# Layer 0's expert network in 240 pieces between the attention's steps, in a two-layer transformer kernel

## The chip, the cores and the metric

The kernel runs on one core of one Trainium2 chip. The metric is the device time of one execution in microseconds (us). TensorE (PE) multiplies, its weight loads (PEld) overlap its products; VectorE (DVE), ScalarE (ACT) and GpSimd (POOL) work on what it leaves; SP issues most DMAs. A line number L1673 is a line of the kernel before; L1673 is the helper in which nearly every product is issued, so TensorE's rows are told apart by their tiles.

## The reference, cut to what matters

Two layers act on x of 2 x 1024 tokens of 128 values. Each normalises x, computes an attention s and an expert network g from the same normalised xn, and adds s * silu(g). Layer 0, cut:

```python
xn = _layernorm(x, axis=-1)
s = _L0_attn_ref(xn, ...)     # 16 heads of 8, 1024 x 1024 scores, relative bias, softmax, projection
g = _silu(_L0_ffn_ref(xn, ...))
x = x + s * g
# the expert network: 2 shared experts and 8 routed ones, all computed for all tokens,
# 128 -> 256 -> 128, the routed ones weighted with the top-2 gate
def _ffn(x, w1, w2, w3):
    return jax.nn.silu(x @ w1.T) * (x @ w3.T) @ w2.T
```

Layer 1 has another attention and a larger expert network, which the change doesn't touch but for the numbers of banks, written as a table by layer.

## The kernel before

**Layout.** Features lie on the 128 partitions, tokens along the free axis; `xnT` holds xn so, in four chunks of 512 tokens. PSUM has 8 banks of 512 float32 per partition.

**Start (L1964 to L1972).** Transposes, the projections to q, k and v, and the router. q and k are split into three bf16 parts each and stored to DRAM by SP (`store_qk`, L563), from where stacks of 48 rows (six part-by-part products of 8) are loaded per group of four heads (`load_stacks`, `load_group`). Meanwhile VectorE makes the bias rows (L1520 to L1527, stored at L657) and the gate (L1530 to L1533).

**The expert stage (L2013 on TensorE).** Ten experts in order, each over the four chunks, with two halves of 128 hidden values: 8 units per expert, 80 in all. A unit is `up` (L1975): for w1 and for w3 three float32r products (high by high, high by low, low by high) of 512 columns in two banks, of four in use; ScalarE's Silu of the first (L1002); VectorE's product with the second (L1548); for routed experts GpSimd's product with the gate row (L867); and `down` (L1984), a float32 product added in one of banks 4 to 7, one per chunk. At unit 4 of each expert ScalarE and VectorE split the next expert's weights (L1006, L1515). The loops are `ffn_experts` (L497) on all engines. At the end ScalarE takes Silu of the four banks into `n1T` (L1014).

**The attention (`attention(0)` on each engine).** Two batches with four groups of four heads are eight groups; each is done in two halves H of 512 queries, 16 halves in all. It needs two passes. The *score units* (S) compute 128 queries by 512 keys and VectorE takes their maximum (L1442); 32 of them per half. They go through a ring of banks 0 to 3 (`RING`, `ring_unit` at L1767). When a half's maxima are complete (mark K, L1434), GpSimd splits them in parts (L810 to L813), TensorE transposes them (unit M), VectorE copies them (L1447) and SP writes them as three more rows of the q stack (`max_rows`, L597). The *transposed pass* of a half has 8 steps of 128 keys: per step four products T (128 keys by 512 queries, one per head, `st_step`) with 51 rows, in banks 4 to 6 in turn, whose exponential ScalarE takes (L943), and the value product of the step before (`av_step`, eight float32 passes into four column groups of bank 7). Heads alternate between array rows 0 to 63 and 64 to 127. For some query tiles the bias is added by small bf16 products (`s_adds`, `st_adds`, with `flip`).

The order is written out by a planner (`s_stream`, `s_plan`, L117 to L169): 52 score units and a K and an M come before the first step (`first_units`), and the others are dealt over the steps, those of later halves into the steps of earlier ones. Within a step TensorE issues T and a share of the units for each of the four heads, and the value product behind the third T. All engines run the same lists in order; waits are on counters (`ring_full`, `ring_free`, `st_ps`, `e_done`, `av_done`).

After each half the sums go out and back through DRAM (`sums_out`, `sums_back`, SP) and GpSimd multiplies (`normalise`, L819). SP's order of this is `attention_feed` (L623). In the last half, without score units, TensorE begins the output projection (`first_projection`, L1906); VectorE's `projected` (L1556) multiplies it by `n1T` and adds it to xT.

Of the kernel before, what the change touches and what calls it, by code (L numbers as in the profile page):

```python
# [51 lines left out]
RING = 4  # L52
EXP = 8
FFN_SEQ = EXP + 2
REL = 249
# [32 lines left out]
def s_units(layer, H):  # L88
# [10 lines left out]
    return out  # L99

# [119 lines left out]
def block_net(nc, a, out):  # L220
    ctx = ExitStack()
    with ctx:
# [13 lines left out]
        drev_dram = dram("drev_dram", (GROUPS, HG, 2, PARTS, DREV), BF16)  # L236
# [44 lines left out]
        with ExitStack() as over:  # L281
# [3 lines left out]
            part("below_x_hi", 8, F32)  # L285
            x_hi = part("x_hi", 8)
            part("below_x_lo", 8, F32)
            x_lo = part("x_lo", 8)
            part("below_xe", 32, F32)
# [5 lines left out]
            part("below_g", 4, F32)  # L295
            g_hi_lo = part("g_hi_lo", 16)
# [11 lines left out]
        q_at = [4 * G for G in range(GROUPS)]  # L308
        k_at = [48, 52, 56, 60, 32, 36, 40, 44]
        Qs = [bf(k, 4).rearrange("p (r t) -> p r t", r=PAIRS) for k in q_at]  # L310
        Ks = [bf(k, 4).rearrange("p (r t) -> p r t", r=PAIRS) for k in k_at]
# [12 lines left out]
        lrow = at(140, 2)  # L324
# [14 lines left out]
        def gate_bufs(n):  # L339
# [14 lines left out]
        cwb = at(100, 16).rearrange("p (s t) -> p s t", s=2)  # L354
        fw0 = fw[:, 0:1536].rearrange("p (s n) -> p s n", s=2)
        fa = fw[:, 2048:3072].rearrange("p (s n) -> p s n", s=2)
        fg = fw[:, 3072:5120].rearrange("p (s n) -> p s n", s=4)
        x_r = [x_hi, x_lo]
        g_r = [g_hi_lo[:, 2048 * h:2048 * (h + 1)].rearrange("p (s n) -> p s n", s=4) for h in range(2)]
        w_r = w_hi_lo[:, :].rearrange("p (s h n) -> p s h n", s=2, h=2)  # L360
# [34 lines left out]
        w_in, router_in, late_in, fw_in, tbl_in = (sem(n) for n in ("w_in", "router_in", "late_in", "fw_in", "tbl_in"))  # L395
        zero_done, const_done, ones_set = sem("zero_done"), sem("const_done"), sem("ones_set")
# [9 lines left out]
        drev_ready, drev_stored = sem("drev_ready"), sem("drev_stored")  # L406
# [4 lines left out]
        sq_ready, gate_exp, gneg = sem("sq_ready"), sem("gate_exp"), sem("gneg")  # L411
        last_sums, last_norm = sem("last_sums"), sem("last_norm")

        f_w = [sem(f"f_w{s}") for s in range(2)]
        f_c = [sem(f"f_c{s}") for s in range(2)]
        h_ps, a_made, g_made, gw_made, y_done, y_ev = (sem(n) for n in ("h_ps", "a_made", "g_made", "gw_made", "y_done", "y_ev"))
        xhi_made, xlo_made, whi_made, wlo_made, ghi_made, glo_made = (sem(n) for n in (
            "xhi_made", "xlo_made", "whi_made", "wlo_made", "ghi_made", "glo_made"))
# [21 lines left out]
        for l in range(2):  # L440
            first_part, planned = s_plan(l)
            first_units.append(first_part)
            unit_plan.append(planned)
            where, count = ring_of(l)
            place.append(where)
            n_units.append(count)

# [49 lines left out]
        def ffn_experts(eng, expert, chain=None, per=0):  # L497

            expert(0, 0, 0, 0, 0)
            expert(1, 0, 8, 1, 1)
            with eng.Fori(0, 3) as it:
                if chain:
                    chain.enter(it, per)
                expert(it * 2 + 2, it * 16, 16, 0, 2)
                expert(it * 2 + 3, it * 16, 24, 1, 2)
            if chain:
                chain.leave(3)  # L510
            expert(8, 0, 64, 0, 2)
            expert(9, 0, 72, 1, 3)

        def load_group(eng, l, G, pieces=range(4)):


            for piece in pieces:
                hh = piece // 2
                dr, rows, at_ = ((q_dram[l], ROWS, q_at), (k_dram[l], TROWS, k_at))[piece % 2]
# [5 lines left out]
        def proj_weights(eng, n, name):  # L525
            eng.dma_start(fw[:, n * 1024:(n + 1) * 1024].rearrange("p (e c) -> p e c", e=EXP),
                          a["L1_ffn_" + name].rearrange("e c h -> c e h")).then_inc(fw_in, 16)

# [4 lines left out]
        def _(sp):  # L533
# [13 lines left out]
            sp.dma_start(tblr[:, :], a["bias_rev_T"]).then_inc(tbl_in, 16)  # L547
# [205 lines left out]
        def _(pool):  # L753
# [105 lines left out]
            def gate_units(n, n_term, base, slot, kind):  # L859
                if kind in (0, 3):  # L860
                    return
# [1383 lines left out]
```

## Time and profile before

| | |
|---|---|
| times of 3 runs | 1247.46, 1248.37, 1251.16 us, median 1248.37 |
| span of the profiled execution | 1246.1 us (its own time outside the profile isn't given; the median lies 2.3 above the span) |
| instructions | 19644, of which 7308 products |
| mean granted TensorE clock | 0.919 |
| HBM read, written | 61.32 MB, 14.61 MB |

How to read it: the span goes from the first to the last instruction. A busy share is a mean over stages with different limits. Ends of products are modelled, so two that overlap in the trace may be one stream behind another; distances between starts are the safer reading. "Idle before" is the time in which an engine had nothing, with who ended it; TensorE's waits show at its weight loads.

### The profile page before, as it was taken

What the parts mean: (1) busy time and instruction counts of PE and PEld (TensorE: products, weight loads), DVE (VectorE), ACT (ScalarE), POOL (GpSimd) and SP (SyncE); (2) the same over time, 40 slices, a digit from 0 to 9 for tenths busy, and PEclk for the clock granted to TensorE, in tenths of its full rate; (3) what the DMA queues carried; (4) which work ended last, traced back from release to release, by engine and by line L of the source; (5) the groups of instructions that cost most, each with busy time, mean ns of one, the idle gap of its engine ahead of it and who ended that gap; (6) DMA issues with size and microseconds to landing.
All of it is one profiled execution on the core that took longest, in us unless ns stands there. A gap on an engine that the chain in (4) does not pass through costs nothing.

```text
span 1246.1 us, 19644 instructions
## 1 busy us (share of the span) xinstructions
PE 1097.0 (88%) x7308; PEld 516.1 (41%) x7308; DVE 815.6 (65%) x1631; ACT 648.9 (52%) x1257; POOL 193.2 (16%) x313
## 2 busy tenths in 40 slices
PE   6499999789999999999994589899999999897777
PEld 4366666322222222222232244434444467553444
DVE  5633333488998998898257678787876156546654
ACT  4323323217777787787742227566777533433434
POOL 2135555000100111011100001112221000001000
PEclk9699999859999999999987559889999999998888
DMA  4612213311112111010005302211233020000331
GB/s 117 218 47 93 93 60 96 103 28 27 46 49 51 43 37 45 16 39 12 19 1 178 98 21 76 64 56 47 85 105 122 18 77 1 1 1 0 137 136 34
DMA packets 62470, 77.79 MB, mean 62 GB/s; under 512 B 15836, under 2 KB 40108, under 8 KB 60588
## 3 DMA queue, kind: packets, MB, share of 16 engines
q1 hardware_dynamic: 53592, 65.34, 16.7%
q10 hardware_dynamic: 8788, 11.26, 3.1%
q8 instruction: 56, 0.92, 0.3%
q14 instruction: 34, 0.28, 0.1%
HBM read 61.32 MB, written 14.61 MB: 61 GB/s over the span
## 4 chain that ended last, share of the span: by engine, by line
PE 65%; DVE 20%; ACT 7%; SPq 3%; issue 3%; DMA 2%; ACTq 0%; POOL 0%; DVEq 0%
PE PS L1673 63%; DVE mx L1442 10%; ACT arena L943 5%; SPq L587 2%; SPq L595 1%; DMA arena<-drev_dram 1%; PE PS L1686 1%; DVE arena L1241 1%; DVE arena L1647 1%; DVE arena L1244 1%; DMA arena<-mrow 0%; DVE arena L1205 0%; DVE arena L1193 0%; DMA arena<-in_L_attn_x 0%; DVE small L1633 0%
## 5 line engine op out<-in xcount | busy, mean ns | idle before, releaser
L1673 PE MATMUL PS<-arena 128*32 128x512 f32 (+13 forms) x3656 | 606.4, 479 | 70.7 <-DVE mx L1442 20.7
L1442 DVE TENSOR_REDUCE mx<-PS 128x1 f32<-128x512 f32 (+3 forms) x896 | 500.5, 624 | 95.5 <-PE PS L1673 94.9
L943 ACT ACTIVATE arena<-PS 128x512 f32<-128x512 f32 (+3 forms) x896 | 438.3, 556 | 230.3 <-PE PS L1673 223.1
L1673 PEld LDWEIGHTS PS<-arena 128*32 128x32 f32 (+3 forms) x3656 | 159.0, 104 | 439.2 <-DVE mx L1442 175.2
L1673 PE MATMUL PS<-x_hi,w_hi_lo 128*128 128x512 f32 x320 | 145.1, 495 | 0.8 <-DVE combT L1305 0.4
L1548 DVE TENSOR_TENSOR fw<-PS,fw 128x512 f32<-128x512 f32 x80 | 55.3, 692 | 119.7 <-ACT fw L1002 117.9
L1002 ACT ACTIVATE fw<-PS 128x512 f32<-128x512 f32 x80 | 47.8, 597 | 123.5 <-PE PS L1673 123.5
L867 POOL TENSOR_TENSOR fw<-fw,arena 128x512 f32<-128x512 f32 x64 | 84.9, 1327 | 88.8 <-DVE fw L1548 88.8
L1673 PE MATMUL PS<-fw 128*128 128x512 f32 (+3 forms) x184 | 90.3, 578 | 0.0
L819 POOL TENSOR_TENSOR arena<-arena,fw 128x512 f32<-128x512 f32 x31 | 40.0, 1290 | 275.6 <-DMA fw<-sum_dram 275.6
L1673 PEld LDWEIGHTS PS<-x_hi,w_hi_lo 128*128 128x128 f32 x320 | 61.2, 191 | 31.1 <-issue 19.4
L1673 PE MATMUL PS<-arena,fw 128*128 128x512 f32 x128 | 68.0, 651 | 5.2 <-DVE arena L1629 5.2
L1673 PE MATMUL PS<-x_lo,w_hi_lo 128*128 128x512 f32 x160 | 63.9, 399 | 0.0
L1673 PE MATMUL PS<-identb_sw,mask_kq_sw 64*128 64x128 bf16 x256 | 56.1, 238 | 0.0
L1673 PE MATMUL PS<-identb,mask_kq 64*128 64x128 bf16 x256 | 54.4, 238 | 0.0
L810 POOL CAST mparts<-mneg 128x16 bf16<-128x16 f32 x24 | 4.7, 196 | 316.5 <-DVE mneg L1435 316.5
L1673 PE MATMUL PS<-mask_kq_sw,identb_sw 64*128 64x128 bf16 x256 | 53.1, 224 | 0.0
L1673 PE MATMUL PS<-mask_kq,identb 64*128 64x128 bf16 x256 | 52.1, 224 | 0.0
L1673 PE MATMUL PS<-e_hi_lo,w_hi_lo 128*128 128x512 f32 x144 | 45.3, 395 | 0.0
L1673 PE MATMUL PS<-e_hi_lo,fw_lo 128*128 128x512 f32 x104 | 41.1, 395 | 0.0
L1659 DVE TENSOR_TENSOR arena<-arena 128x512 f32<-128x512 f32 x32 | 22.0, 697 | 27.2 <-ACT arena L1172 27.2
L1673 PEld LDWEIGHTS PS<-x_lo,w_hi_lo 128*128 128x128 f32 x160 | 30.7, 192 | 22.1 <-issue 18.3
(313 smaller groups left out, 1113.9 us busy)
## 6 DMA issues: line engine op xcount, KB each, us to landing
arena<-comb_dram SPq DMA_DIRECT2D x14, 1024.0 KB, 5.0
arena<-comb_dram SPq DMA_DIRECT2D x18, 512.0 KB, 7.3
fw<-sum_dram SPq DMA_DIRECT2D x31, 256.0 KB
q_dram<-arena SPq DMA_DIRECT2D x24, 256.0 KB, 3.7
k_dram<-arena SPq DMA_DIRECT2D x24, 256.0 KB, 3.9
arena<-drev_dram SPq DMA_DIRECT2D x32, 192.0 KB, 4.3
arena<-k_dram ACTq DMA_DIRECT2D x20, 204.0 KB
fw<-in_ffn_w SPq DMA_DIRECT2D x10, 384.0 KB, 3.2
```

The source lines that it names most:

```text
L587: sp.dma_start(dst, src).then_inc(att[l][f"ld{n}"], 16)
L595: sp.dma_start(Hst[row:row + 64, parity, j // 2, :, :], src).then_inc(h_ld[parity], 16)
L819: g.tensor_tensor(OT[:, G, 512 * h:512 * (h + 1)], Osb[:, h, :], RB[l][:, h, :], ALU.mult).then_inc(A["r_done"], 1)
L867: g.tensor_tensor(g_, g_, cwb[:, slot, 512 * (u // 2):512 * (u // 2 + 1)], ALU.mult).then_inc(gw_made, 1)
L943: s.activation(Pr[:, m % 8, 0:w], bank(4 + m % 3, 0, w), ACT.Exp).then_inc(A["e_done"], 1)
L1002: s.activation(fa[:, u % 2, :], bank(2 * (u % 2)), ACT.Silu).then_inc(a_made, 1)
L1241: v.tensor_tensor(src, src, dst[:, 0, :], ALU.subtract).then_inc(rest_done, 1)
L1244: v.tensor_tensor(dst[:, 2, :], src, dst[:, 1, :], ALU.subtract).then_inc(split_done, 1)
L1442: v.reduce_max(mx[:, H % 2, kh, n:n + 1], bank(U % RING, 0, w), axis=AX.X, negate=True).then_inc(A["ring_free"], 1)
L1548: v.tensor_tensor(fg[:, u % 4, :], bank(2 * (u % 2) + 1), fa[:, u % 2, :], ALU.mult).then_inc(g_made, 1)
L1659: v.tensor_tensor(gg[:, U % 4, :], ga[:, U % 4, :], rwb[e][:, chunk(2 * b + c)], ALU.mult).then_inc(i_g, 1)
L1673: return nc.tensor.matmul(out_, lhsT, rhs, start=start, stop=stop)
```

## The change

The expert stage goes. Its 80 units k are now ordered by chunk first (20 per chunk), and each is cut in three pieces: A (three products with w1 into bank 2), B (three with w3 into bank 3) and D (the down product into bank 6, two units later). Two pieces stand behind each four of the first 52 score units, in 13 parts of the lead; the other 214 are dealt evenly behind the 120 steps of halves 0 to 14. The score ring of layer 0 has banks 0 and 1, T has banks 4 and 5. The value product of the step before stands ahead of the third T, no longer behind it.

Silu is made as x/2 * (1 + tanh(x/2)): ScalarE takes Tanh and a halved Copy of bank 2, VectorE combines (tanh + 1) * bank 3, GpSimd multiplies the halved copy by the gate row (routed experts) and the two together, and splits the low part of the weights. Per chunk the sum gets Tanh on ScalarE and one more operation on VectorE; the missing 0.5 is in `projected`. The stacks of layer 0 lie in four slots (group G in slot G mod 4) and are loaded group by group, the second batch inside the attention; ScalarE's queue stores the second batch's q and k. The bias rows are made ahead of the projections and stored once, not once per batch. The loops of `ffn_experts` are gone: all is unrolled. Core of the diff:

```diff
-RING = 4
+RINGS = (2, 4)
+ST_BANKS = (2, 3)
+UNITS = 2 * FFN_SEQ * NC
+FFN_LAG = 2
+LEAD_PIECES = 2
+def ffn_pieces():
+    pieces = []
+    for k in range(UNITS):
+        pieces += [("A", k), ("B", k)]
+        if k >= FFN_LAG:
+            pieces.append(("D", k - FFN_LAG))
+    return pieces + [("D", k) for k in range(UNITS - FFN_LAG, UNITS)]
...
# SP: one feed for layer 0, the expert loads between its parts
+                for H in range(HALVES):
+                    for i in range(KT):
+                        if i == 1 and H >= 1:
+                            sums_out(0, H - 1)
+                        if i == 1 and H % 2 == 1 and H // 2 + 2 < GROUPS:
+                            sp.wait_ge(A["st_ps"], HG * steps_before(0, H))
+                            load_bias(H // 2 + 2)
+                        if i == 4 and H >= 1:
+                            sums_back(0, H - 1)
+                        expert_loads((H, i))
+                        if ("M", H + 1) in unit_plan[0][H][i]:
+                            max_rows(0, H + 1)
...
# GpSimd
+                    if kind == "A":
+                        if routed(q):
+                            r = gate_index(q)
+                            pool.wait_ge(f_c[r % 2], 16 * (r // 2 + 1))
+                            pool.wait_ge(h1_out, k + 1)
+                            own.link(g.tensor_tensor(fh[:, k % 2, :], fh[:, k % 2, :], cwb[:, r % 2, :], ALU.mult))
+                        if k % 2 == 0 and q + 1 < UNITS // 2:
+                            weights_lo(q + 1)
+                    if kind == "B":
+                        pool.wait_ge(h1_out, k + 1)
+                        pool.wait_ge(u_made, k + 1)
+                        g.tensor_tensor(fu[:, k % 4, :], fu[:, k % 4, :], fh[:, k % 2, :], ALU.mult).then_inc(g_made, 1)
...
# ScalarE, behind the exponentials of a step
+                    if kind == "A":
+                        act.wait_ge(h1_ps, k + 1)
+                        if k >= 2:
+                            act.wait_ge(u_made, k - 1)
+                            act.wait_ge(g_made, k - 1)
+                        s.activation(ft[:, k % 2, :], bank(2), ACT.Tanh, scale=0.5).then_inc(t_made, 1)
+                        s.activation(fh[:, k % 2, :], bank(2), ACT.Copy, scale=0.5).then_inc(h1_out, 1)
+                        if k % 2 == 0 and k // 2 + 1 < UNITS // 2:
+                            weights_hi(k // 2 + 1)
...
# VectorE, behind the maxima of a step
+                    if kind == "B":
+                        dve.wait_ge(h3_ps, k + 1)
+                        dve.wait_ge(t_made, k + 1)
+                        if k >= 4:
+                            dve.wait_ge(y_done, k - 3)
+                        v.scalar_tensor_tensor(fu[:, k % 4, :], ft[:, k % 2, :], 1.0, bank(3), ALU.add, ALU.mult).then_inc(u_made, 1)
...
# TensorE
-                    if m >= 3:
-                        pe.wait_ge(A["e_done"], m - 2)
+                    if m >= ST_BANKS[l]:
+                        pe.wait_ge(A["e_done"], m - ST_BANKS[l] + 1)
...
                         for j in range(HG):
+                            if l == 0 and j == 2 and before:
+                                av_step(*before)
                             st_step(H, i, j)
-                            if j == 2 and before:
+                            if l == 1 and j == 2 and before:
                                 av_step(*before)
...
                         before = (H, i)
+                        if l == 0:
+                            expert_pieces((H, i))
...
+                    if kind == "A":
+                        if k % 2 == 0:
+                            pe.wait_ge(wlo_made, q + 1)
+                        if first:
+                            pe.wait_ge(xlo_made, c + 1)
+                        if k:
+                            pe.wait_ge(h1_out, k)
+                        split_mm(bank(2), [w_r[:, q % 2, h, col:col + 128] for h in range(2)],
+                                 [x_r[h][:, chunk(c)] for h in range(2)]).then_inc(h1_ps, 1)
```

## Rows read from the trace of the kernel before

**Rows 1.** The page, part 1: engine, busy us, share, instructions.

```profile
span 1246.1 us, 19644 instructions
PE 1097.0 (88%) x7308; PEld 516.1 (41%) x7308; DVE 815.6 (65%) x1631; ACT 648.9 (52%) x1257; POOL 193.2 (16%) x313
```

**Rows 2.** Windows: expert stage, lead, 15 halves, last half; clock, DMA share, GB/s.

```profile
core 0: us, PE busy (x) PEld busy (x) DVE busy (x) ACT busy (x) POOL busy (x), PEclk, DMA share, GB/s
51.00:233.50 182.50, 182.04 (x639) 121.88 (x640) 61.25 (x93) 53.71 (x90) 85.70 (x67) 0.98 0.25 81
233.50:272.90 39.40, 27.23 (x101) 6.14 (x99) 28.98 (x50) 3.35 (x5) 1.18 (x5) 0.55 0.16 47
272.90:609.60 336.70, 314.19 (x2821) 87.55 (x2821) 289.99 (x509) 259.92 (x494) 32.68 (x80) 0.99 0.14 37
609.60:630.00 20.40, 20.30 (x102) 6.13 (x98) 6.67 (x19) 12.99 (x26) 1.27 (x1) 1.00 0.05 15
```

**Rows 3.** Groups of 51 to 233.5: busy us, mean ns, idle before and releaser.

```profile
L867 POOL TENSOR_TENSOR fw<-fw,arena 128x512 f32<-128x512 f32 x64 | 84.9, 1327 | 88.8 <-DVE fw L1548 88.8
...
L1548 DVE TENSOR_TENSOR fw<-PS,fw 128x512 f32<-128x512 f32 x80 | 55.3, 692 | 119.7 <-ACT fw L1002 117.9 <-PE PS L1673 1.8
L1002 ACT ACTIVATE fw<-PS 128x512 f32<-128x512 f32 x80 | 47.8, 597 | 123.5 <-PE PS L1673 123.5
...
L1002 ACT ACT_TABLE_LOAD x1 | 1.3, 1283 | 5.2 <-PE PS L1673 5.2
```

**Rows 4.** Timeline of the expert stage: start us, us. The down product of three units.

```profile
62.01 1.02 PE L1673 MATMUL PS<-fw 128*128 128x512 f32 x2
...
64.25 1.02 PE L1673 MATMUL PS<-fw 128*128 128x512 f32 x2
...
66.50 1.02 PE L1673 MATMUL PS<-fw 128*128 128x512 f32 x2
```

**Rows 5.** The chain that ended last, in the lead: start us, us, what.

```profile
223.21 7.36 SPq L595
230.61 2.87 SPq L595
233.53 4.29 SPq L595
237.86 14.00 DMA arena<-drev_dram
...
264.20 4.19 DVE mx L1442 x7
```

**Rows 6.** Groups of 363.5 to 586.5, ten halves.

```profile
L1442 DVE TENSOR_REDUCE mx<-PS 128x1 f32<-128x512 f32 x321 | 196.4, 680 | 24.3 <-PE PS L1673 24.3
...
L1673 PEld LDWEIGHTS PS<-arena 51*128 51x128 bf16 x320 | 23.9, 94 | 44.0 <-ACT arena L943 36.6 <-issue 4.2
L1673 PEld LDWEIGHTS PS<-arena 48*128 48x128 bf16 x320 | 22.0, 94 | 85.6 <-DVE mx L1442 62.3 <-issue 18.8
```

**Rows 7.** Timeline of a step: T's, value's and S's weight loads, and the maxima.

```profile
596.54 1.89 DVE L1442 TENSOR_REDUCE mx<-PS 128x1 f32<-128x512 f32 x3 [0.75 <-PE PS L1673]
596.98 0.09 PEld L1673 LDWEIGHTS PS<-arena 51*128 51x128 bf16 x1 [0.53 <-ACT arena L943]
597.29 0.16 PEld L1673 LDWEIGHTS PS<-arena 128*32 128x32 f32 x8 [0.23 <-issue]
598.29 0.33 PEld L1673 LDWEIGHTS PS<-arena 48*128 48x128 bf16 x5 [0.84 <-DVE mx L1442]
598.72 1.29 DVE L1442 TENSOR_REDUCE mx<-PS 128x1 f32<-128x512 f32 x2 [0.28 <-PE PS L1673]
```

**Rows 8.** Timeline of another step: a bias pair, four products, the exponentials.

```profile
396.98 0.24 PE L1673 MATMUL PS<-arena,flip 64*64 64x128 bf16 x1
...
397.34 0.60 PE L1673 MATMUL PS<-arena 51*128 51x512 bf16 x4
...
397.75 1.58 ACT L943 ACTIVATE arena<-PS 128x512 f32<-128x512 f32 x3 [0.90 <-PE PS L1673]
...
398.41 0.95 PE L1673 MATMUL PS<-arena 51*128 51x512 bf16 x5 [0.47 <-ACT arena L943]
```

**Rows 9.** SP's queue after the projections: start us, issue us.

```profile
36.31 4.75 SPq L571 DMA_DIRECT2D q_dram<-arena  x6
41.10 4.62 SPq L578 DMA_DIRECT2D k_dram<-arena  x6
...
54.82 0.35 SPq L671 DMA_DIRECT2D arena<-comb_dram  x1
```

**Rows 10.** The source line of VectorE's combination with PSUM: ns min, median, max.

```profile
L1560 DVE SCALAR_TENSOR_TENSOR n1T<-PS,cols,n1T x4: 743/748/752, 617.3 to 657.2; 128x512 f32<-128x512 f32 x4
```

More of the change, by code:

```diff
@@ L99, in s_units, with lead_parts, ffn_places @@
     return out
+def lead_parts(first):
+    parts, n = [[]], 0
+    for what in first:
+        if what[0] == "S" and n == 4:
+            parts.append([])
+            n = 0
+        n += what[0] == "S"
+        parts[-1].append(what)
+    return parts
+def ffn_pieces():
[5 more added lines that the diff above has]
+    return pieces + [("D", k) for k in range(UNITS - FFN_LAG, UNITS)]
+def ffn_places(lead):
+    pieces, at_ = ffn_pieces(), {}
+    for n in range(lead):
+        at_["L", n] = [pieces.pop(0) for _ in range(LEAD_PIECES)]
+    places = [(H, i) for H in range(HALVES - 1) for i in range(KT)]
+    done, total = 0, len(pieces)
+    for n, place in enumerate(places):
+        upto = total * (n + 1) // len(places)
+        at_[place] = pieces[done:upto]
+        done = upto
+    return at_
 LAG = (1, 2)
@@ L294, in block_net @@
             w12_hi = part("w12_hi", 8)
[L295 to L296 removed]
+            part("below_g", 20, F32)
             w_hi_lo = part("w_hi_lo", 12)
@@ L821, in attention @@
                 stage(0)
+                if l == 0:
+                    for n, part in enumerate(lead):
+                        if ("K", 0) in part:
+                            max_parts(0)
+                        gate_units(("L", n))
+                    for H in range(HALVES):
+                        for i in range(KT):
+                            if i == 1 and H % 2 == 0 and H // 2 + 1 < GROUPS:
+                                stage(H // 2 + 1)
+                            if ("K", H + 1) in unit_plan[0][H][i]:
+                                max_parts(H + 1)
+                            if i == 6 and H >= 1:
+                                normalise(H - 1)
+                            gate_units((H, i))
+                    return
                 for H in range(LAG[l]):
@@ L930, in attention @@
                     loads[-1]()
+                if l == 0:
+                    for n in range(len(lead)):
+                        gate_halves(("L", n))
                 for H in range(HALVES):
@@ L1459, in attention @@
                 if l == 0:
-                    sequence(first_units[l])
+                    for n, part in enumerate(lead):
+                        sequence(part)
+                        ffn_units(("L", n))
                 else:
@@ L1970, in _ @@
             pe.wait_ge(k_ev, 4)
[L1971 removed]
+            pe.wait_ge(router_in, 32)
             gate_rows(0, xnT, 0, 2)
[L1975 to L1982 removed]
@@ L2012, in _ @@
             pe.wait_ge(v_ev, 4)
-            ffn_experts(pe, ffn_expert)
-            for u in range(8 - LAG, 8):
-                down(72, u, 1, False, False, True)
             attention(0)
```

447 lines of the change are left out of this document (215 added, 232 removed).

## The prediction

> **What bounds the kernel now.** I read the page's busy shares first, then a table of windows, then groups and timelines inside each window. TensorE is busy 88% of the span [rows 1], but the windows show that this is the sum of stages with different limits [rows 2]. The expert network of layer 0 takes 51.0 to 233.5, 182.5 us, and there TensorE is busy 182.04 us while VectorE and ScalarE stand at a third. The reader is to see in [rows 3] that they wait for TensorE (123.5 us) and not the reverse. One unit (3 + 3 products and the down product) starts every 2.24 us [rows 4], and 80 units are 179 us. So this stage is TensorE's stream.
>
> Then comes the attention's lead, 233.5 to 272.9, 39.4 us at a granted clock of 0.55, with TensorE busy 27.2 us. The chain runs through SP's queue and a bias load of 14.0 us and then through VectorE's maxima [rows 5]. Then 15 halves take 272.9 to 609.6, 336.7 us or 22.45 each, and a last half without score units 20.4 [rows 2]. In ten of these halves VectorE is busy with 321 maxima for 196.4 us [rows 6], in steady state one per 0.60 us (1.89 us for three, [rows 7]); 32 of them are 19.3 us. TensorE is only a little looser.
>
> **TensorE's own step.** Products of 48 or 51 rows start 0.22 us apart, and two in different halves of the array start together (four in 0.60 us, [rows 8]). The value product starts 0.31 us after the last of them and the next score product 1.00 us after it [rows 7]. A step (T, S with T, S, T, value, S with T, S) is 3 x 0.22 + 0.31 + 1.00 + 2 x 0.22 = 2.41 us, the same as VectorE's 4 x 0.60. Eight steps are 19.3; in each half two steps have two score units only, -0.9; the bias products are about 0.36 us for each of four pairs (396.98 to 397.34, [rows 8]) and nearly 2 us in the two steps of the transposed side, 3.4 in a group of two halves, +1.7. So TensorE needs 20.1 us of the 22.45. This is the centre of the argument: **the stage into which the experts are moved has about 2.3 us per half free on TensorE, not 22**.
>
> **The change, part by part.** The profiled execution has a span of 1246.1 us; the median of the runs is 1248.4, 2.3 above, which I add at the end.
>
> Removed: the stage, -182.5.
>
> The lead: 52 score units in 13 parts of four, with two expert pieces behind each, 26 of the 240. With a ring of two, a third score product waits for the first maximum: product to maximum 0.43 us (598.29 to 598.72, [rows 7]), the maximum 0.69, the release 0.06. A part is about 1.1 (third unit) + 0.6 (fourth) + 1.36 (two pieces at 3 x 0.23) + 0.4, near 3.5 us, since the combining operation of VectorE stands between the maxima. 13 x 3.5 = 45.5, with the bias pairs 49. The stack loads and the bias load now lie beside the gate's chain and the first 20 units, so their stall of 10 us goes. 49 - 39.4 = +9.6. The start stays near 51: the gate's chain on VectorE begins some 3.5 us earlier, but ScalarE now issues twelve stores (4.75 + 4.62 us on SP's queue, [rows 9]) ahead of the gate's exponential.
>
> The 15 halves get 214 pieces, 14.3 each or 4.76 units: 4.76 x 2.24 = +10.65 on TensorE. Each step also goes from 64-row tiles to the whole array and back once more. The value product's entry costs 0.31 - 0.22 = 0.09 and its exit 1.00 less twice 0.44 (mean 604 ns less the 0.16 by which a modelled end passes its stream), 0.12; 8 x 0.2 = +1.6. The Trainium skill (TensorEngine Tiling (Array Packing), Key Properties) says that a change of tiling mode drains the engine. By that rule this is a real cost and the trace agrees, with 0.09 and 0.12 us; without it the sum would be 24 us lower.
>
> So TensorE's own work is 20.1 + 10.65 + 1.6 = 32.4 us per half. VectorE has 19.3 + 4.8 combinations + small ones = 23.5, ScalarE (259.9 us / 15 = 17.3, [rows 2]) + 4.8 x 1.1 (tanh and copy) + 2.4 x 0.5 = 23.8, GpSimd about 12 products of 1.33 us [rows 3], 2.4 weight splits and the normalisation, 20. **TensorE becomes the bound**, and what counts is how often it waits in order:
> - Two steps of each half have six score units. Now the third stands behind a two-bank ring: it can start 0.22 + 0.43 + 0.69 + 0.06 = 1.4 us into the step, not 0.66, and the last one waits again for the maximum of the second before it, about 0.6. 2 x 1.4 = 2.8 us.
> - T has two banks, so the third T of a step waits for the first exponential. That loop is 0.41 (397.34 to 397.75) + 0.60 + 0.06 [rows 8], 1.1 us, covered by 1.6 us of work. But 38 of 120 steps end in an A piece, whose tanh and copy (0.60 and 0.49 more) ScalarE does before the next exponential, in 19 of them with a weight copy of 0.5. The third T is then 0.3 or 0.8 us late, the fourth 0.27 more. 2.5 steps per half x 0.8 = 2.0, of which a third falls into the steps above: 1.3.
> - The bias pairs need both banks of a ring at once: 0.4.
> Together 4.5, so 36.9 us per half: 15 x (36.9 - 22.45) = +217.
>
> The last half has two T banks: its third T waits 1.1 us, behind 1.5 of other work, +1.5 at most. Half 14 has four steps without score units, -2. The final sum needs tanh and two VectorE operations per chunk, three times hidden by the steps, and at the end far ahead of the projection: 0. The bias strips are stored once, not twice, six DMAs less on SP; no wait on it is seen in the attention: 0.
>
> Operations the trace lacks: tanh from PSUM has Silu's 0.597 us as its nearest row and the exponential's 0.60; I take 0.60 (between 0.56 and 0.75, 0.2 us per half on an engine that isn't the bound). VectorE's combination from PSUM lies between 0.692 (L1548) and 0.748 (L1560), [rows 3, 10]; 0.75. The SP loads in the loop (0.35 us each, [rows 9]) are 10 a half beside some 6 us of its own: between nothing and 1 us per half if a max-row load comes late; I take 0. GpSimd beside VectorE: no difference is seen in the expert stage, 0, upper bound 0.5 us per half.
>
> Sum: -182.5 + 9.6 + 217 + 1.5 - 2 = +43.6; 1246.1 + 43.6 + 2.3 = 1292. I state **1290**. The point of balance is 22.45 + (182.5 - 9.6 + 0.5)/15 = 34.0 us per half.
>
> **The rivals.**
> (a) The pieces fill the gaps. Waits on VectorE and on ScalarE (62.3 and 36.6 us ahead of weight loads in ten halves, [rows 6]) are where a piece that is ready could stand. If the two-bank waits fall together with them, a half is 30.75 (no switch cost) to 33.4 (with it and 1 us): -182.5 + 9.6 + 125 to 164 - 0.5 = -48 to -9, so 1200 to 1239, mid 1222. For it: both other engines are under 24 us. Against it: TensorE is in order, and the waits come behind pieces that are placed at the end of a step only.
> (b) Slower, by one mechanism at one place: the two-bank ring at the six-unit steps and the exponentials behind tanh. This is the forecast's own 4.5 us; it decides from 1.6 us per half on (34.0 - 32.4). At 7 us it gives 15 x 2.5 more, 1328.
> (c) Tables. If tanh and the exponential didn't share a table, each A piece would load twice: a load is 1.28 us [rows 3], 160 loads are 205 us on ScalarE, 14 us per half beside 23.8, so 38 with every wait behind it, some 1290 + 120 = 1410. The Trainium skill (ScalarE: Activation LUTs, Table sets: the hidden batching unit) lists tanh in the exponential's set, and by that rule this rival is nothing; no row of this trace holds a tanh.
> (d) GpSimd is late: each routed unit needs two products of 1.33 us and half a split, 3.3 us of the 7.7 us between units. It decides only if the maxima's parts queue behind them for over two steps, +1 us per half, 1305. That the change does not do what it says can't be: the order is written out.
>
> **How the numbers follow.** Forecast 0.60, with (b)'s worse half in it; (a) 0.28; between them, 1240 to 1255, 0.07; (c) 0.02; (d) 0.03. The range leaves out the best part of (a) and (c): 1218 to 1328. The forecast's own range is 1262 to 1328. About 0.3% (3.7 us) is what a measurement of this kernel can tell from no change. Faster 0.30, same 0.06, slower 0.64.
>
> **What would show it.** The 15 halves take 36 to 38 us each, in all some 550 (34.0 is balance); the first step starts near 100 us, and the last projection some 43 us later than now. TensorE's waits name VectorE's maxima in the six-unit steps and the exponential at the third T. No table load between 60 and 650 us. A half at 31 to 33 us, or a lead under 40, would prove me wrong; so would a clock under 0.95 in the steps, or long waits for GpSimd.

## The result, and the profile of the changed kernel

The changed kernel takes 1321.0 us (1318.1 to 1329.7, four runs), the kernel before 1249.8 beside it: a ratio of 1.0575, 95% interval 1.0527 to 1.0623. It is slower by 71 us, where the prediction had 42, and inside the forecast's own range of 1262 to 1328. The profiled execution has a span of 1320.4 us against 1246.1.

Part 1 of the page of the changed kernel, for [rows 1], with the first line of the page:

```profile
span 1320.4 us, 19956 instructions
PE 1135.2 (86%) x7308; PEld 502.6 (38%) x7308; DVE 828.9 (63%) x1625; ACT 704.5 (53%) x1365; POOL 339.5 (26%) x433
```

TensorE is about as busy, by share, as it was; this tells nothing of where 74 us went. The windows do, cut at the same places as [rows 2]: the lead, the 15 halves, the last half, and then two single halves.

```profile
core 0: us, PE busy (x) PEld busy (x) DVE busy (x) ACT busy (x) POOL busy (x), PEclk, DMA share, GB/s
56.90:116.60 59.70, 47.28 (x170) 20.33 (x170) 37.69 (x61) 12.46 (x23) 25.63 (x27) 0.78 0.31 80
116.60:679.10 562.50, 515.30 (x3393) 183.96 (x3392) 354.60 (x580) 358.85 (x674) 239.53 (x245) 0.99 0.22 61
679.10:702.00 22.90, 22.08 (x106) 6.50 (x104) 8.04 (x23) 15.30 (x28) 1.27 (x1) 1.00 0.04 13
159.50:195.30 35.80, 32.98 (x193) 11.53 (x191) 25.03 (x41) 24.59 (x48) 17.57 (x18) 1.00 0.28 73
195.30:234.00 38.70, 35.19 (x263) 12.95 (x263) 24.07 (x40) 24.48 (x48) 12.17 (x13) 1.00 0.19 54
```

The 15 halves took 336.7 us and take 562.5, 37.5 each. In a half VectorE and ScalarE are busy about 24 us each and GpSimd 12 to 18: none of them fills it. VectorE's 23.6 and ScalarE's 23.9 us per half are what the prediction counted (23.5 and 23.8); GpSimd's 16.0 is less than its 20. TensorE is busy 515.3 of 562.5, so at least 47 us are gaps of its own, and more where the modelled end of a product covers a short wait. The groups of this stretch show who waits for whom:

```profile
L1544 DVE TENSOR_REDUCE mx<-PS 128x1 f32<-128x512 f32 x462 | 296.7, 685 | 157.1 <-PE PS L1775 156.8
L1033 ACT ACTIVATE arena<-PS 128x512 f32<-128x512 f32 x480 | 261.8, 597 | 149.7 <-PE PS L1775 148.8 <-issue 0.6
L1650 DVE SCALAR_TENSOR_TENSOR fw<-fw,PS 128x512 f32<-128x512 f32 x71 | 48.7, 686 | 30.8 <-PE PS L1775 29.5
L1081 ACT ACTIVATE fw<-PS 128x512 f32<-128x512 f32 x71 | 42.4, 597 | 51.6 <-PE PS L1775 50.8
L1775 PEld LDWEIGHTS PS<-arena 48*128 48x128 bf16 x462 | 34.5, 95 | 73.1 <-DVE mx L1544 60.8 <-issue 11.4
L1775 PEld LDWEIGHTS PS<-arena 51*128 51x128 bf16 x482 | 32.5, 93 | 189.5 <-ACT arena L1033 124.8 <-issue 64.5
```

The maxima (first line) used to wait 24.3 us in ten halves [rows 6] and now wait 156.8 in 15: VectorE has become the one that waits. The last two lines are what TensorE's loads wait for. The line of ScalarE's exponentials is the larger one and has doubled in weight: 36.6 us in ten halves before, 124.8 in 15 now, 3.7 and 8.3 per half. Such a list says who came last before TensorE went on, not what it would gain without that wait; the experiments below put the larger price on the maxima. The Tanh (L1081, 597 ns) takes exactly what Silu took [rows 3], and no table load lies among the steps. So rival (c) is out. The Trainium skill (ScalarE: Activation LUTs, Table sets: the hidden batching unit) puts Tanh in the exponential's set, and the trace agrees, with none of the 160 loads of 1.28 us that the rival counted.

A step with six score units of the changed kernel, at a granted clock of 1.00: VectorE's maxima, and two of TensorE's loads for score units (start us, duration us):

```profile
460.06 1.29 DVE L1544 TENSOR_REDUCE mx<-PS 128x1 f32<-128x512 f32 x2 [0.50 <-PE PS L1775]
462.49 1.29 DVE L1544 TENSOR_REDUCE mx<-PS 128x1 f32<-128x512 f32 x2 [1.14 <-PE PS L1775]
464.92 1.29 DVE L1544 TENSOR_REDUCE mx<-PS 128x1 f32<-128x512 f32 x2 [1.14 <-PE PS L1775]
...
461.40 0.09 PEld L1775 LDWEIGHTS PS<-arena 48*128 48x128 bf16 x1 [0.44 <-DVE mx L1544]
463.83 0.09 PEld L1775 LDWEIGHTS PS<-arena 48*128 48x128 bf16 x1 [0.34 <-DVE mx L1544]
```

Where [rows 7] has a run of three maxima and then two more 0.28 us later, they now come in pairs, as the ring of two gives them, with 1.1 us of nothing between pairs, and TensorE waits for them inside the step, as forecast. Last, the start. SP's queue, then the first entries that TensorE and VectorE have of the lead, in the chain that ended last:

```profile
41.37 1.19 SPq L744
...
42.68 0.91 SPq L564
...
44.98 11.74 DMA arena<-k_dram
...
56.86 0.63 PE PS L1775 x2
57.49 0.69 DVE mx L1544
...
58.23 4.07 PE PS L1775 x8
...
62.32 0.69 DVE fw L1650
63.01 1.21 DVE mx L1544 x2
```

The first group's stack loads (L564, four issues) stand on SP behind the bias stores (L744), and the last of them lands 11.7 us after its issue. Until then the lead can't begin: it begins at 56.9, not near 51. In the last two lines the maxima stand behind the combination of an expert unit on VectorE (0.69 us), and with them the banks that TensorE waits for.

The split of the whole span, by three marks in each trace: the first score product, the first transposed product, and ScalarE's evacuation of the value sums of half 14 and of half 15 (2.5 us after the end of a half as cut in [rows 2]). The last column but one is all the rest, which is layer 1 and the output.

| kernel | first score product at | lead | to evacuation 14 | to 15 | rest | span |
|---|---|---|---|---|---|---|
| before | 234.0 | 39.0 | 339.1 | 28.6 | 605.4 | 1246.1 |
| after | 56.9 | 59.8 | 565.0 | 30.4 | 608.3 | 1320.4 |

The forecast had 51.5, 48.6, 554.1, 30.1 and 605.4 in this order. It missed 5.4, 11.2, 10.9, 0.3 and 2.9 us, all to the same side, so no error of one stage hid that of another.

### The profile page after: what moved, and what is told of

Read it like the earlier page. It is cut to its first block, busy times and chain, and to the rows that moved or that the text cites. A ratio compares the mean times of both kernels' runs of the same rounds, so it can differ in the third digit from the quotient of the medians.

```text
span 1320.4 us, 19956 instructions
## 1 busy us (share of the span) xinstructions
PE 1135.2 (86%) x7308; PEld 502.6 (38%) x7308; DVE 828.9 (63%) x1625; ACT 704.5 (53%) x1365; POOL 339.5 (26%) x433
## 4 chain that ended last, share of the span: by engine, by line
PE 72%; DVE 14%; ACT 7%; issue 3%; DMA 2%; SPq 1%; ACTq 0%; POOL 0%; DVEq 0%
PE PS L1775 70%; DVE mx L1544 7%; ACT arena L1033 3%; PE PS L1788 1%; ACT arena L1082 1%; DMA arena<-k_dram 1%; ACT w_hi_lo L1070 1%; DVE arena L1343 1%; DVE arena L1749 1%; DVE fw L1650 0%; SPq L744 0%; DVE arena L1307 0%; SPq L585 0%; PE PS L2199 0%; DVE arena L1295 0%
## 5 line engine op out<-in xcount | busy, mean ns | idle before, releaser
L1775 PE MATMUL PS<-arena 128*32 128x512 f32 (+13 forms) x3656 | 624.6, 480 | 104.9 <-DVE mx L1544 61.1
L1544 DVE TENSOR_REDUCE mx<-PS 128x1 f32<-128x512 f32 (+3 forms) x896 | 515.3, 626 | 225.5 <-PE PS L1775 224.4
L1033 ACT ACTIVATE arena<-PS 128x512 f32<-128x512 f32 (+3 forms) x896 | 447.2, 554 | 270.6 <-PE PS L1775 266.3
L1775 PE MATMUL PS<-x_hi,w_hi_lo 128*128 128x512 f32 x320 | 148.1, 482 | 0.0
L948 POOL TENSOR_TENSOR arena<-arena 128x512 f32<-128x512 f32 x64 | 81.3, 1271 | 194.6 <-ACT arena L1082 194.6
L954 POOL TENSOR_TENSOR fw<-fw,arena 128x512 f32<-128x512 f32 x80 | 101.6, 1270 | 114.8 <-DVE fw L1650 113.5
L1081 ACT ACTIVATE fw<-PS 128x512 f32<-128x512 f32 x80 | 47.8, 597 | 102.8 <-PE PS L1775 102.0
L1775 PE MATMUL PS<-fw 128*128 128x512 f32 (+3 forms) x184 | 99.4, 628 | 0.0
L1650 DVE SCALAR_TENSOR_TENSOR fw<-fw,PS 128x512 f32<-128x512 f32 x80 | 54.9, 686 | 39.0 <-PE PS L1775 37.6
L936 POOL TENSOR_TENSOR w_hi_lo<-fw,w_hi_lo 128x512 fp32r<-128x512 f32 x40 | 50.8, 1271 | 31.6 <-ACT w_hi_lo L1070 29.2
L1082 ACT ACTIVATE arena<-PS 128x512 f32<-128x512 f32 x80 | 47.4, 592 | 0.0
```

The lines of the kernel that those rows point to most:

```text
L936: g.tensor_tensor(w_r[:, q % 2, 1, :], w13[:, q % 2, :], w_r[:, q % 2, 0, :], ALU.subtract).then_inc(wlo_made, 1)
L948: own.link(g.tensor_tensor(fh[:, k % 2, :], fh[:, k % 2, :], cwb[:, r % 2, :], ALU.mult))
L954: g.tensor_tensor(fu[:, k % 4, :], fu[:, k % 4, :], fh[:, k % 2, :], ALU.mult).then_inc(g_made, 1)
L1033: s.activation(Pr[:, m % 8, 0:w], bank(4 + m % ST_BANKS[l], 0, w), ACT.Exp).then_inc(A["e_done"], 1)
L1081: s.activation(ft[:, k % 2, :], bank(2), ACT.Tanh, scale=0.5).then_inc(t_made, 1)
L1082: s.activation(fh[:, k % 2, :], bank(2), ACT.Copy, scale=0.5).then_inc(h1_out, 1)
```

## The experiments

**Rings or pieces.** Is a half long because of the small rings, or because TensorE has more to do in it? A kernel that does all 240 pieces in one block ahead of the lead, and has the rings of the changed kernel in an attention without pieces; and the same block with the rings of before.

```diff
 def ffn_places(lead):
+    return {("P", 0): ffn_pieces()}
...
                 if l == 0:
+                    expert_pieces(("P", 0))
+                    pe.wait_ge(u_made, UNITS)
...
```

The other engines take that place at the head of the attention too, and TensorE waits there for the last results of the block.

> All 240 pieces stand in one block ahead of the lead; the attention keeps the change's two ring banks, two T banks and place of the value product. My theory (37.3 us per half are 20 of TensorE's own, 10.7 of pieces, 1.6 of array switches and about 5 of waits that the two-bank rings and the tanh cause together): the rings alone cost some 2 us a half, so the 15 halves take 24 to 25.5 us each. Rival 'rings': the small rings cost nearly all of the waits without any piece in between, 27 us or more per half. Rival 'pieces': the rings cost nothing, 22.4 as before.

> As the one before, but with four ring banks and three T banks again (free once the block is done). All theories: 22.4 to 22.7 us per half as in the kernel before; above 23 the earlier value product or the ring of stacks costs something that neither counts.

Measured, one run each: 1469.7 us with rings of 2 and 2, 1328.5 with 4 and 3. The windows, columns as above: first with the small rings the lead, two halves at full clock and one at a low clock:

```profile
310.60:351.30 40.70, 31.50 (x98) 6.65 (x98) 31.45 (x50) 0.00 (x0) 1.18 (x5) 0.50 0.05 18
394.10:422.70 28.60, 22.96 (x154) 5.47 (x153) 20.85 (x36) 18.03 (x35) 2.50 (x6) 1.00 0.22 55
422.70:452.00 29.30, 24.30 (x227) 7.04 (x225) 20.47 (x35) 17.74 (x34) 2.10 (x5) 1.00 0.09 27
613.10:653.20 40.10, 36.74 (x227) 7.96 (x225) 21.08 (x36) 17.85 (x35) 2.10 (x5) 0.60 0.06 18
```

Then with the large rings the block, the lead and two halves:

```profile
51.00:312.00 261.00, 203.67 (x641) 115.32 (x642) 58.73 (x89) 109.50 (x203) 230.58 (x186) 0.96 0.35 100
312.00:342.30 30.30, 28.13 (x99) 6.17 (x99) 28.85 (x50) 0.00 (x0) 1.18 (x5) 0.55 0.08 25
488.40:512.10 23.70, 21.93 (x228) 6.49 (x226) 20.39 (x37) 17.22 (x34) 2.11 (x5) 1.00 0.12 36
512.10:534.00 21.90, 20.17 (x156) 4.89 (x152) 19.87 (x35) 17.21 (x34) 2.52 (x6) 1.00 0.26 65
```

TensorE's longest wait in that block:

```profile
PEld PS L1780 <- POOL w_hi_lo L939: 83.9, 39, 8.2
```

At the full clock, a half is 28.6 and 29.3 us with the small rings and 21.9 and 23.7 with the large ones: 28.95 against 22.8. **The rings by themselves cost 6.2 us per half**, three times what I had expected of them, and what the rival 'rings' said. The large rings give 22.8 where the kernel before has 22.45, so what else the change brings to the attention (the earlier value product, the ring of stacks) costs little; over all 15 halves it is 350.1 us to evacuation 14 against 339.1, 4 of these 11 us in the first half, whose granted clock is 0.64 and was 0.81. The small rings cost the lead 10.4 us as well (40.7 against 30.3). With 28.95 as the base, 14.3 pieces and the switches (10.65 + 1.6 by the prediction) would give 41.2, and the changed kernel has 37.5. By this sum some 3.7 us per half of the pieces do go into gaps, as rival (a) said, but into gaps that the same change has made; no single run shows the 3.7. The block itself takes 261 us and not the stage's 182.5 because GpSimd is busy 230.6 in it and TensorE's loads wait 83.9 us for the weights that GpSimd splits: rival (d)'s price is real there, at 2.9 us of GpSimd per unit (230.6 / 80), where (d) had 3.3 for a routed one. It is covered as soon as the pieces stand among the steps, where TensorE's loads wait 1.2 us for GpSimd in 15 halves.

**Which of the two rings.** One ring enlarged at a time, in the block form: that of the scores in one kernel, that of T in the other.

```diff
-RINGS = (2, 4)
+RINGS = (4, 4)
```

```diff
-ST_BANKS = (2, 3)
+ST_BANKS = (3, 3)
```

> The block form with four ring banks and two T banks, to split the 6.2 us per half (28.6 to 29.3 at full clock against 21.9 and 23.7) that both small rings cost together without a piece in between. Theory 'score ring': the six-unit steps and the pairs do it, so this one takes 23 to 24.5 us per half. Theory 'T banks': the third T behind the exponential does it, so this one takes 26 or more.

> The block form with two ring banks and three T banks. Theory 'score ring': 27 us or more per half. Theory 'T banks': 23 to 25. If both this and the other take 25 to 26.5, the costs add and neither ring is the cause alone.

Measured, one run each: 1380.4 and 1436.7 us. Two halves at full clock, first with the score ring alone enlarged:

```profile
481.20:506.30 25.10, 21.66 (x155) 4.86 (x153) 20.59 (x36) 17.94 (x34) 2.51 (x6) 1.00 0.21 57
506.30:533.00 26.70, 23.19 (x227) 6.91 (x225) 20.59 (x36) 17.79 (x35) 2.11 (x5) 1.00 0.10 31
```

And with the T ring alone enlarged:

```profile
573.10:601.40 28.30, 21.89 (x156) 5.19 (x153) 20.72 (x36) 17.43 (x34) 2.50 (x6) 1.00 0.19 52
601.40:630.00 28.60, 23.83 (x227) 6.68 (x225) 20.22 (x35) 17.36 (x34) 2.11 (x5) 1.00 0.09 27
```

Against 22.8 the T ring of two alone costs 3.1 us per half (25.9), the score ring of two alone 5.7 (28.45), both 6.2. They don't add, and nor do the whole stretches to evacuation 14, lower clocks included (51, 101 and 129 us over 350.1). The likely reason is that while TensorE waits for a maximum, the exponential that it would wait for next gets done; that is argued, not shown. The first expectation missed on both theories (25.9 lies between them), the second held for the score ring (27 or more). The score ring is the larger cost.

**The six-unit steps and the place of D.** The plan weighs K and M units, so two steps of a half get six score units and others two. With weight 0 for them all steps have four. And apart from that: the down product last in its place, so that 8 steps end in an A piece and not 38.

```diff
+        weight = (lambda x: cost(x) if x[0] == "S" else 0) if layer == 0 else cost
-            done += cost(what)
+            done += weight(what)
```

```diff
-    return at_
+    return {place: sorted(part, key=lambda x: x[0] == "D") for place, part in at_.items()}
```

> The change with marks K and M weighing nothing in layer 0's plan, so that every step has four score units and none has six. My theory: the waits of the two steps with six units, 2 x 1.4 us a half, go, and the two steps with two units get 0.44 each: 1.5 to 2.8 us less per half, 22 to 40 us less in all, about 1285 to 1298. Rival (the waits sit in other steps): under 8 us less.

> The change with the down product D last among the pieces of its place, so that tanh and copy start 0.9 us earlier where a place ended in A. My theory: about 1 us less per half, 10 to 20 us less in all, near 1305. Rival (the exponentials behind tanh are not what TensorE waits for): within 4 us of the change.

> The change with even steps and D last together. If the two act on different waits they add: 1320 - 41 - 18 in the span, about 1262. If they are the same wait seen twice: 1272 to 1280.

Measured: 1278.5 us (ratio 1.0239, 1.0167 to 1.0311), 1305.0 (1.045, 1.0398 to 1.0503) and for both 1265.0 (1.013, 1.0094 to 1.0166). The first is faster than was expected (1285 to 1298), the other two are as expected.

| kernel | first score product at | lead | to evacuation 14 | to 15 | rest | span |
|---|---|---|---|---|---|---|
| four score units in each step | 57.6 | 59.5 | 524.8 | 30.4 | 607.3 | 1279.6 |
| D last | 55.9 | 59.6 | 547.3 | 30.2 | 609.0 | 1302.0 |
| both | 57.1 | 61.8 | 507.1 | 30.4 | 604.3 | 1260.7 |

In the 15 halves the even steps are worth 40.2 us (2.7 per half), D last 17.7 (1.2; the prediction's term is 1.3), and both 57.9 (3.9), so the two act on different waits. Both waits are where the prediction had them, and D last has its size. For the even steps the comparison needs care. The prediction takes 0.9 us off a half because two steps have two score units only, so with four in each its own work is 33.3 and not 32.4, and the term of 2.8 should give back 1.9 net; it gave 2.7. The missing 0.8 is near the 4 x 0.22 us that the four extra units of the six-unit steps take by the prediction's own spacing, and that it counted nowhere; no run separates it. What is left of a half is (507.1 - 2.5) / 15 = 33.6, against 33.3 of TensorE's own work, and the windows show hardly a gap: TensorE is busy 501.7 of 507.1.

```profile
118.90:626.00 507.10, 501.69 (x3405) 184.60 (x3405) 353.46 (x581) 363.05 (x678) 240.21 (x245) 1.00 0.25 68
```

**A piece earlier in the step.** If pieces fill gaps, one should stand where the gap is: the first piece of a place goes ahead of the value product, the others stay at the end.

```diff
+                            if l == 0 and j == 2:
+                                expert_pieces((H, i), slice(0, 1))
                             if l == 0 and j == 2 and before:
                                 av_step(*before)
...
-                            expert_pieces((H, i))
+                            expert_pieces((H, i), slice(1, None))
```

> As the one before, and the first piece of each step stands ahead of the value product and not behind the step. Theory (what is left are waits for exponentials and maxima at the third T and third S, into which a piece fits): 1 to 2 us less per half than with even steps and D last, 1235 to 1250. Rival (the piece only moves the wait, since ScalarE and VectorE still do its follow-up behind the whole step): within 5 us of it.

Measured: 1299.1 us (1.0362, 1.0259 to 1.0466), 34 more than the kernel without this edit; the part to evacuation 14 is 544.4 against 507.1. Both theories missed. The list of waits of the 15 halves (us in total, times, longest), for this kernel:

```profile
ACT arena L1034 <- PE PS L1776: 190.2, 172, 2.1
...
DVE mx L1545 <- PE PS L1776: 154.9, 133, 2.4
PEld PS L1776 <- ACT arena L1034: 150.7, 238, 1.0
```

And for the one without the edit:

```profile
PEld PS L1776 <- ACT arena L1034: 134.6, 182, 1.5
...
ACT arena L1034 <- PE PS L1776: 119.5, 175, 2.2
DVE mx L1545 <- PE PS L1776: 112.4, 178, 1.7
```

ScalarE waits 71 us more for TensorE and VectorE 42 us more, and TensorE waits for ScalarE 238 times, not 182. A piece between the second and the third T may starve both engines that release the banks, so that the releases come late for TensorE. This chain of causes is argued from the list; which link weighs most was not tried.

**The lead.** It has 50 score units (462 of the 512 stand in the steps), not 52 as the plan was described: 12 parts of four and one of two. Now 25 parts of two score units and one piece, 25 pieces in the lead and not 26; then also the first stack load ahead of the bias stores on SP.

```diff
-LEAD_PIECES = 2
+LEAD_PIECES = 1
-        if what[0] == "S" and n == 4:
+        if what[0] == "S" and n == 2:
```

```diff
+            sp.wait_ge(qk_stored[0][0], 16 * 12)
+            load_group(sp, 0, 0)
             sp.wait_ge(setup_done, 1)
             for part in range(PARTS):
...
-            load_group(sp, 0, 0)
             sp.wait_ge(drev_stored, 16 * PARTS * 2)
```

> Even steps and D last, and the lead in 26 parts of two score units with one piece behind each, not 13 of four with two. My theory of the lead (62 us from the first score unit to the first step, where 49 were forecast: the third unit of a part waits for a maximum behind VectorE's combination, and half of the parts run at a granted clock of 0.5): a piece now stands where that wait was, so the lead takes 48 to 54 us and the whole 1250 to 1258. Rival (TensorE's stream at the low clock is all of it): the lead stays within 3 us of 62.

> As the one before, and SP loads the first group's stacks ahead of the bias stores. In the change they are issued from 42.7 and the first score unit starts at 56.9 after a landing of 11.7 us. Theory (the stores' issue is ahead of it, and their packets beside it): it starts 3 to 6 us earlier and so does all that follows. Rival (the landing waits for ScalarE's twelve stores and the projections' own): under 1.5 us.

Measured: 1256.6 us (1.0073, 1.0051 to 1.0096) and 1266.5 (1.0137, 1.0036 to 1.0238, two runs of 1257.2 and 1275.8). The pairs take the lead from 61.8 to 49.6 us, as expected (48 to 54); the span gains 9.3: with a ring of two, a part of four waits in its own middle. The earlier load moved the first score product by 1.6 us only, to 55.8, near the rival's 1.5, and the lead took 54.7. Its chain shows why there was little to gain:

```profile
35.80 5.96 DMA k_dram<-arena
...
41.84 0.33 SPq L565
```

The loads read what the stores of q and k have written, and those land at 41.8, so the loads went out at 41.84 and not at 42.68. The profiled execution of this kernel is 18 us longer in layer 1, where the edit changes nothing, so its total says nothing of the edit; the expected 3 to 6 us are not seen.

The split of these and of the next two kernels:

| kernel | first score product at | lead | to evacuation 14 | to 15 | rest | span |
|---|---|---|---|---|---|---|
| lead in pairs | 57.4 | 49.6 | 509.2 | 30.2 | 605.0 | 1251.4 |
| and first load earlier | 55.8 | 54.7 | 510.7 | 30.3 | 622.5 | 1274.0 |
| and rounding on GpSimd | 55.9 | 52.0 | 504.0 | 30.4 | 604.4 | 1246.8 |
| and 37 pieces in the lead | 54.5 | 64.5 | 499.3 | 30.2 | 605.1 | 1253.6 |

**Relief for ScalarE.** Together with all of the above, GpSimd and no longer ScalarE rounds the high part of the weights.

```diff
+                    g.tensor_copy(w_r[:, q % 2, 0, :], w13[:, q % 2, :]).then_inc(whi_made, 1)
...
-                        if k % 2 == 0 and k // 2 + 1 < UNITS // 2:
-                            weights_hi(k // 2 + 1)
```

> As the one before, and GpSimd makes the high part of the weights too, so that ScalarE has one copy less behind an A piece. Theory (exponentials behind tanh, copy and weight copy hold TensorE's third T): 0.3 us per half, 3 to 6 us in all, 1242 to 1250. Rival (GpSimd, which is busy 43% of the steps, makes the weights late): 3 us or more slower than the one before.

Measured over ten runs: 1248.4 us, 0.9997 (0.9971 to 1.0023): no difference from the kernel before. Lead and 15 halves:

```profile
55.90:108.00 52.10, 45.67 (x169) 18.56 (x170) 37.05 (x61) 9.77 (x18) 28.43 (x31) 0.85 0.42 109
108.00:612.00 504.00, 500.47 (x3408) 185.26 (x3408) 353.33 (x582) 349.35 (x644) 260.72 (x280) 1.00 0.25 68
```

That is within what was expected (1242 to 1250). ScalarE has 13.7 us less to do than with the even steps and D last (363.05 to 349.35), and the stretch to evacuation 14 is 3 to 7 us shorter than in the three kernels that lead to this one (507.1, 509.2, 510.7; these differ by 3.6 among themselves with nearly the same steps, one profiled execution each). A half takes 33.4 us, against the 33.3 of own work worked out above. TensorE's busy time, 500.5 of 504.0, can't show by itself that no wait is left: the changed kernel was busy 515.3 us with the same products, so busy time has waits in it.

**More pieces in the lead.** If the steps are TensorE's own work and the lead has room, pieces should be moved there. One and two pieces in turn behind the 25 parts, 37 instead of 25 (the expectation counts 26 parts and 39), on top of the last kernel.

```diff
-        at_["L", n] = [pieces.pop(0) for _ in range(LEAD_PIECES)]
+        at_["L", n] = [pieces.pop(0) for _ in range(LEAD_PIECES + n % 2)]
```

> As k_all, with one and two pieces in turn behind the 26 parts of the lead: 39 pieces there and 201 in the steps. Theory (the steps are at TensorE's own work now, 33.6 us per half with 32.4 counted, so a unit taken out of them is worth its 2.24 us, while the lead still has TensorE idle beside VectorE's maxima): the steps take 10 us less, the lead 2 to 6 more, and the whole is 4 to 8 us below k_all, 1240 to 1245, just faster than the kernel before. Rival (the lead is full too, by GpSimd's products or by the low clock): the lead grows by 8 to 14 us and the time stays within 3 us of 1248.

Measured over twelve runs: 1256.6 us, 1.0042 (1.0009 to 1.0075). The theory missed; the rival hit the lead, though not the total. The lead grows by 12.5 us (52.0 to 64.5), the halves shrink by 4.7: 12 pieces cost 1.04 us each in the lead and give back 0.39 each in the steps, half of the 0.75 (2.24 / 3) that they take in TensorE's stream. So the steps don't simply follow TensorE's own work. Part of this is a side effect: 13 steps now end in an A piece, not 6, and by the gain of D last (17.7 us for 30 such steps) that costs an estimated 4 us. The windows, and two of the waits in the lead:

```profile
54.50:119.00 64.50, 54.74 (x200) 24.82 (x200) 39.85 (x65) 14.11 (x26) 41.11 (x42) 0.84 0.40 104
119.00:618.30 499.30, 494.23 (x3376) 180.63 (x3376) 352.68 (x579) 344.93 (x637) 247.74 (x269) 1.00 0.25 66
```

```profile
PEld PS L1779 <- DVE mx L1548: 10.7, 16, 1.5
PEld PS L1779 <- POOL w_hi_lo L942: 8.1, 2, 4.1
```

TensorE waits 10.7 us for maxima, and twice some 4 us for weights that GpSimd splits late. The lead has no room either. A lead without any pieces was planned and has no time: as it was written, a load of q could run ahead of the store of q, so it was never run, and what the lead's pieces cost as a whole stays open.

No kernel of these beats the one before.

## Why the prediction was right, and where it was off

**What bounds each stage: right.** The stage was TensorE's stream, and the attention had little free on TensorE: 2.3 us per half by the prediction, some 1.4 with the 0.9 for the extra units of the six-unit steps. The centre of the argument stands: the best form of the change that I ran has 33.4 us per half ((504.0 - 2.5) / 15), against 33.3 of TensorE's own, and with a lead 13 us longer than before it comes out even, beside a point of balance stated as 34.0. That TensorE's own work is what holds the last form is a match of sums; the run that took 12 pieces out of the steps gave back 4.7 us where their stream is 9.0, and near 9 only with the estimate above added.

**The waits per half: right in sum, 5.1 for 4.5 (37.5 - 32.4).** The exponentials behind an A piece are 1.2 for 1.3, the six-unit steps 2.7 net where the terms give 1.9 (2.8 less 0.9); both are shown by removing each. The term that was mis-sized is, by the prediction's own spacing, TensorE's 20.1: it has the 0.9 that two-unit steps save and not the 0.9 that six-unit steps add. With it own work is 33.3 and the waits are 4.2 for 4.5. What is then left of the even form (33.6) is 0.3, for bias pairs priced at 0.4; 0.2 to 0.45 per half goes with ScalarE's weight copies, hardly more than single executions differ by. What I had wrong is the make-up below it. I took it that without pieces the small rings would cost little; they cost 6.2, and the pieces then fill a part of that. The step that failed is "the waits come behind pieces that are placed at the end of a step only": the pieces at the end give VectorE and ScalarE time to empty their banks. It had little effect on the sum, it seems, since the waits' terms were worked out with the pieces in place. That the two meet within 0.6 us is in part luck: what the rings cost and what the pieces fill were not in the working as such.

**The half's total: 37.5 for 36.9**, with half 14's saving of 2 us in the mean of 37.5. 10.9 us of the error.

**The lead: 59.8 for 48.6, the largest error, 11.2 us.** The term "near 3.5 us" per part was timed at full clock. The granted clock in the lead of the changed kernel:

```profile
56.00:62.00 6.00, 4.38 (x10) 2.15 (x10) 2.58 (x4) 0.90 (x2) 0.86 (x3) 0.50 0.50 140
62.00:70.00 8.00, 5.64 (x20) 2.81 (x20) 6.17 (x10) 2.24 (x5) 3.76 (x3) 0.93 0.94 189
77.00:88.00 11.00, 7.68 (x46) 3.53 (x47) 8.19 (x14) 2.24 (x5) 4.86 (x5) 1.00 0.19 60
97.00:102.00 5.00, 4.16 (x10) 2.02 (x9) 2.82 (x6) 1.60 (x3) 1.82 (x4) 0.50 0.23 77
```

It goes between 2.4 and 1.2 GHz (1.00 and 0.50) and back. A part of four units takes 3.7 to 5.0 us at the first and 5.4 to 6.4 at the second; four of the twelve ran at the second from end to end or nearly, an estimated 6 to 7 us in all. The lead of before was at 0.55 [rows 2], and I priced the pieces there with durations of a stage at 0.98. The second error is in the same term: a part of four units on a ring of two waits twice, which the kernel with parts of two shows: 12.2 us less, of which 2.9 are in TensorE's busy time (48.97 to 46.06) and the rest was waiting. Its mean clock is also a little higher, 0.84 for 0.77, so the two errors aren't fully separated.

**The start: 5.4 us late.** "The start stays near 51" looked at the gate's chain and not at the stack load, which now stands behind the bias stores on SP. That it needs 11.7 us is the price I left out. Moving it ahead gave back 1.6 us only, because the loads wait for the stores of q and k to land in any case and then take as long. The landings may be slow because the DMA engines are full: their share is 0.98 to 1.01 in all windows from 31 to 50 us of the changed kernel (the last of them below), with ScalarE's twelve stores of 256 KB each among SP's. The trace shows the two together; no run took the stores away.

```profile
45.00:50.00 5.00, 0.31 (x1) 0.18 (x1) 1.42 (x5) 1.70 (x3) 0.00 (x0) 0.50 1.00 323
```

**The last half +1.9 for +1.5**, and **layer 1 +2.9 for nothing**, at a clock that differs a little from run to run (604.3 to 609.0 us in kernels that leave it as it is, but for the one execution named above): no effect of the change.

**The rivals.** (a) fell: it had 30.75 to 33.4 us per half, the kernel has 37.5, and only three further edits of the steps (even steps, D last, rounding on GpSimd) bring a half to (a)'s upper end. Its middle of 1200 to 1239 is 1220, not 1222. (b), the waits, is the forecast's own part, within its 4.5 to 7. (d) is nothing in the steps (1.2 us of TensorE's waits). The array's mode switches stay unproven as a term of their own: 1.6 us is consistent with 33.4 and 33.6, but no run changes them alone.

## What to carry to other kernels

Before work is moved under another stage, subtract: the room there is what its bound engine has free (here 1.4 to 2.3 us of 22.45), whatever the other engines' shares say, and banks taken from that stage are a price of their own. Removing single waits then brings the time back towards the engine's own work; here that was exactly even. Price a piece at the clock of the stage that it goes to, and look for the queue in front of the new stage's first load.

## What the runs showed of the hardware

- Two small rings do not add: 3.1 us per half for the one, 5.7 for the other, 6.2 for both, on 22.8.
- In the block form with small rings, halves of one kernel ran at granted clocks from 0.60 to 1.00 (40.1 against 29.3 us at the same products); its 15 halves took 477.1 us, not the 434 of 15 at full clock. Over the 15 halves the mean clock was 0.86 with rings of 2 and 2, 0.91 with 2 and 3, 0.96 with 4 and 2, and 0.99 to 1.00 with the pieces among the steps. So TensorE's waits may cost twice; that they are why the clock is lower is not shown.
- A piece of the same work gives back 0.39 us in the steps and costs 1.04 in the lead (12 pieces moved, one profiled execution each), and one piece per step at another place of the step costs 34 us in all.
- Tanh from PSUM, 128 x 512, takes 597 ns, as Silu and the exponential do; VectorE's three-operand form with PSUM 686 ns at the mean, where 0.75 us was taken.
